# A decoder block in fp32: passes over consecutive tokens, and the steps between attention and experts in earlier half units

## The reference, cut to what matters

```python
x = layernorm(x + attention(x))             # 16 heads of 64, softmax over 1024 keys, Wp, bp
x = layernorm(x + memory(ctx, x))           # a shift of rows; 38 rows are a convolution of rate 4
x = layernorm(x + experts(x))               # top-1 of 8 experts, capacity 1024 / 8 tokens a batch

logits = einsum('bnd,de->bne', tokens, Wg); gates = softmax(logits)
mask = one_hot(argmax(gates), 8)
pos = cumsum(mask, axis=1) * mask - mask    # a token beyond its expert's capacity is dropped
h = gelu(expert_rows @ W1[e]); y = h @ W2[e]
```

## Time and profile before

| | |
|---|---|
| median of three runs | 2017.19 us |
| profiled execution, span | 2020.08 us, 2018.3 us |
| mean granted clock of TensorE | 0.967 |
| busy: PE, PEld, DVE, ACT, POOL | 94%, 62%, 59%, 43%, 68% |
| attention, tail | up to 1716.3 us, 302 us |
| PE waits for max_of (L1203), whole span | 30.8 us in 16 waits, the longest 6.9 |

### The profile page before, as it was taken

How to read it: one execution, slowest core, us unless ns; L and a number is a source line. 1 busy time by engine, 2 the same in 40 slices (tenths; PEclk the granted TensorE clock), 3 DMA queues, 4 the chain that set the end, 5 groups by cost and what they waited for, 6 DMA issues and landing times. The chain is left out here.

```text
span 2018.3 us, 30518 instructions
## 1 busy us (share of the span) xinstructions
PE 1896.4 (94%) x11400; PEld 1257.8 (62%) x11400; DVE 1198.5 (59%) x2123; ACT 865.5 (43%) x1118; POOL 1362.7 (68%) x725
## 2 busy tenths in 40 slices
PE   7899999999999999789999999899999997788996
PEld 5555666656666666456666665556666653777886
DVE  5555655656666656656666657656665675454563
ACT  3344444434434454234435443333344532446663
POOL 1687778778667776587667776686667767353553
PEclk8999999999999999899999999899999998887999
DMA  4300000022111100022102000211111101622330
GB/s 141 87 22 17 22 17 27 17 64 78 44 38 42 34 22 17 22 74 89 42 22 64 16 22 17 66 45 48 37 47 34 32 12 58 204 87 84 118 106 32
DMA packets 150093, 104.24 MB, mean 52 GB/s; under 512 B 74044, under 2 KB 136636, under 8 KB 148924
## 3 DMA queue, kind: packets, MB, share of 16 engines
q1 hardware_dynamic: 146876, 93.82, 15.9%
q0 software_dynamic: 3072, 8.46, 1.1%
HBM read 69.15 MB, written 29.43 MB: 49 GB/s over the span
## 5 line engine op out<-in xcount | busy, mean ns | idle before, releaser
L937 POOL TENSOR_TENSOR prob_sum<-prob_sum,probs 128x1024 f32<-128x1024 f32 x384 | 921.8, 2400 | 251.4 <-ACT probs L1147 223.4
L1203 DVE TENSOR_REDUCE max_of<-spare_ps 128x1 f32<-128x512 f32 x1024 | 656.7, 682 | 388.1 <-PE spare_ps L1030 387.5
L1147 ACT ACTIVATE probs<-score_ps 128x1024 f32<-128x1024 f32 x512 | 504.1, 1026 | 719.1 <-PE score_ps L1051 718.9
L1065 PE MATMUL av_ps<-probs,v 128*64 128x512 f32 x2048 | 488.6, 603 | 3.6 <-issue 3.6
L1030 PEld LDWEIGHTS spare_ps<-k_hi,q_hi 64*128 64x128 f32 x1024 | 160.2, 305 | 228.0 <-issue 191.6
L1030 PE MATMUL spare_ps<-k_hi,q_hi 64*128 64x512 f32 x1024 | 262.8, 507 | 31.5 <-DVE max_of L1203 30.8
L1065 PEld LDWEIGHTS av_ps<-probs,v 128*64 128x64 f32 x2048 | 130.4, 136 | 238.7 <-issue 221.6
L933 POOL TENSOR_TENSOR prob_sum<-probs 128x1024 f32<-128x1024 f32 x64 | 152.4, 2381 | 155.3 <-ACT probs L1147 155.3
L1051 PE MATMUL score_ps<-q_hi,k_hi 64*128 64x512 f32 x1024 | 213.2, 411 | 1.1 <-DVE o_in L1236 0.9
L1051 PE MATMUL score_ps<-shift_rows,ones 64*128 64x512 f32 x1024 | 207.3, 399 | 0.0
L1051 PE MATMUL score_ps<-q_hi,k_lo 64*128 64x512 f32 x1024 | 206.2, 396 | 0.0
(11 more groups left out here) (202 smaller groups left out, 2363.6 us busy)
## 6 DMA issues: line engine op xcount, KB each, us to landing
o_transposed<-o_out SPq DMA_DIRECT2D x64, 256.0 KB, 2.1
w_raw<-in_L_ffn_W_dram SPq DMA_DIRECT2D x16, 1024.0 KB, 5.6
o_in<-o_transposed SPq DMA_DIRECT2D x26, 512.0 KB, 4.0
w_raw<-in_L_attn_Wq_dram SPq DMA_DIRECT2D x64, 64.0 KB, 2.3
w_raw<-in_L_attn_Wk_dram SPq DMA_DIRECT2D x64, 64.0 KB, 2.2
wv_raw<-in_L_attn_Wv_dram SPq DMA_DIRECT2D x32, 128.0 KB, 2.8
x<-in_x_dram SPq DMA_DIRECT2D x4, 1024.0 KB, 6.0
xT_kept<-x_transposed SPq DMA_DIRECT2D x4, 1024.0 KB, 6.4
```

Source lines behind the costliest of these rows:

```text
L937: pool.tensor_tensor(out, out, probs[:, n % RING], ALU.add).then_inc(prob_added, 1)
L1065: last = pe.matmul(av_ps[hd * E:(hd + 1) * E, :], v[:, quad % 2, kt, 2 * first_head + hd, :], probs[:, n % RING, hd, :], start=(kt == 0), ...
L1147: act.activation(probs[:, n % RING], score_ps[n % 2][:, :, :], ACT.Exp).then_inc(probs_ready, 1)
L1203: dve.tensor_reduce(max_of[:, u % 2, kh, j, hd:hd + 1], bank[:, :], AX.X, ALU.max).then_inc(pass_read, 1)
```

## The change

Three parts. A pass takes 128 consecutive tokens as weights. The maxima then lie with the token along the partitions, so VectorE transposes them in blocks of 32 (neg_max, now 128 x 32 with zeros behind the eight used columns, into neg_rows, one buffer each) and four DMAs, one for each group of 32 partitions, write runs of 32 tokens into shift_rows. The route's projections come in the half units s = 4 to 11, and all that follows them three half units earlier. find_free and find_rows are cut into five pieces (kept, free, numbers, place, rows) in s = 26 to 28, and the sends stand in s = 29 and s = 30, four each.

```diff
@@ -167,7 +167,7 @@
         self.steps = 0
 
 
-    PROJECTED_AT = (5, 6, 7, 9, 10, 11, 13, 14)
+    PROJECTED_AT = (4, 5, 6, 7, 8, 9, 10, 11)
 
     def add_buffers(self, nc, ctx, more):
 
@@ -183,35 +183,39 @@
         early = {1: [("load_x", b)],
                  2: [("load_o", T0), ("load_o", T0 + 1), ("bias", b, 0)],
                  3: [("bias", b, 1)],
-                 15: [("load_cw", b), ("ids", b), ("load_new", b)],
-                 16: [("norm1", b, 4)],
-                 17: [("old", b), ("norm1", b, 0)],
-                 18: [("move", b), ("moved", b, 0)],
-                 19: [("moved", b, 1)],
-                 22: [("norm2", b, 0)],
-                 23: [("x2T", b, 0), ("norm2", b, 4)],
-                 24: [("x2T", b, 1)],
-                 25: [("x2T", b, 2)],
-                 26: [("x2T", b, 3)],
-                 27: [("choose", b)],
-                 28: [("tally", b)],
-                 29: [("count", b)],
-                 31: [("send", b, 0), ("send", b, 1)]}.get(s, [])
+                 12: [("load_cw", b), ("ids", b), ("load_new", b)],
+                 13: [("norm1", b, 4)],
+                 14: [("old", b), ("norm1", b, 0)],
+                 15: [("move", b), ("moved", b, 0)],
+                 16: [("moved", b, 1)],
+                 19: [("norm2", b, 0)],
+                 20: [("x2T", b, 0), ("norm2", b, 4)],
+                 21: [("x2T", b, 1)],
+                 22: [("x2T", b, 2)],
+                 23: [("x2T", b, 3)],
+                 24: [("choose", b)],
+                 25: [("tally", b)],
+                 26: [("count", b)],
+                 27: [("free", b)],
+                 28: [("place", b)],
+                 29: [("send", b, 0)],
+                 30: [("send", b, 1)]}.get(s, [])
         late = {3: [("split", T0)],
-                15: [("aggr", 0, b), ("scale", 0, b)],
-                16: [("norm1", b, 6)],
-                17: [("norm1", b, 2)],
-                19: [("comp", b), ("stats2", b, 0)],
-                20: [("stats2", b, 1)],
-                21: [("aggr", 1, b), ("scale", 1, b)],
-                22: [("norm2", b, 2)],
-                23: [("logits", b, 0), ("norm2", b, 6)],
-                24: [("logits", b, 1)],
-                25: [("logits", b, 2)],
-                26: [("logits", b, 3)],
-                27: [("mask", b)],
-                29: [("rows", b, 0)],
-                30: [("rows", b, 1)]}.get(s, [])
+                12: [("aggr", 0, b), ("scale", 0, b)],
+                13: [("norm1", b, 6)],
+                14: [("norm1", b, 2)],
+                16: [("comp", b), ("stats2", b, 0)],
+                17: [("stats2", b, 1)],
+                18: [("aggr", 1, b), ("scale", 1, b)],
+                19: [("norm2", b, 2)],
+                20: [("logits", b, 0), ("norm2", b, 6)],
+                21: [("logits", b, 1)],
+                22: [("logits", b, 2)],
+                23: [("logits", b, 3)],
+                24: [("mask", b)],
+                26: [("kept", b)],
+                27: [("numbers", b)],
+                28: [("rows", b)]}.get(s, [])
         for t in range(self.TB):
             early += [("load_o", T0 + t)] if t > 1 and s == (at[t - 3] + 1 if t > 2 else 4) else []
             late += [("proj", T0 + t)] if s == at[t] else []
@@ -559,7 +563,7 @@
         dve.tensor_copy(self.counts[:, :, :], bank[:, 0:(self.TB + 1) * self.EX]
                         .rearrange("p (t e) -> p t e", e=self.EX)).then_inc(self.counts_out, 1)
 
-    def find_free(self, dve, b):
+    def find_kept(self, dve, b):
         CAP, EX = float(self.CAP), self.EX
         base = self.base[:, b, :]
         in_tile, total = self.counts[:, 0:self.TB, :], self.counts[:, self.TB, :]
@@ -570,11 +574,17 @@
                           base.rearrange("p (a e) -> p a e", a=1).broadcast_to([P, self.TB, EX]), ALU.add)
         self.step(dve, dve.scalar_tensor_tensor(out=self.kept[:, :, :], in0=in_tile, scalar=CAP,
                                                 in1=self.mask[:, :, :], op0=ALU.is_lt, op1=ALU.mult))
+
+    def find_free(self, dve, b):
+        CAP, base = float(self.CAP), self.base[:, b, :]
         dve.tensor_scalar(self.free[:, :], self.taken[:, :], -1.0, CAP, ALU.mult, ALU.add)
         dve.tensor_tensor(self.free_row[:, :], self.taken[:, :], base, ALU.add)
         dve.tensor_reduce(self.dropped_before[:, :], self.dropped[:, :, :], AX.X, ALU.add)
         dve.tensor_reduce(self.keep[:, :], self.kept[:, :, :], AX.X, ALU.add)
         self.step(dve, dve.tensor_tensor(self.work[:, :, :], self.number[:, :, :], self.kept[:, :, :], ALU.mult))
+
+    def find_numbers(self, dve, b):
+        EX = self.EX
         dve.tensor_reduce(self.row[:, :], self.work[:, :, :], AX.X, ALU.add)
         dve.tensor_tensor(self.x2[:, :, self.GATE:self.GATE + 1], self.gate[:, :].rearrange("p (t a) -> p t a", a=1),
                           self.keep[:, :].rearrange("p (t a) -> p t a", a=1), ALU.mult)
@@ -583,8 +593,7 @@
                                          ALU.mult))
         self.step(dve, dve.tensor_reduce(self.free_before[:, :], self.triangle[:, :, :], AX.X, ALU.add))
 
-    def find_rows(self, dve, b):
-        tiles = slice(b * self.TB, (b + 1) * self.TB)
+    def find_place(self, dve, b):
         number, inside, work = self.number[:, :, :], self.inside[:, :, :], self.work[:, :, :]
         self.step(dve, dve.tensor_tensor(number, self.spread(self.dropped_before), self.over_tokens(self.free_before),
                                          ALU.subtract))
@@ -594,6 +603,9 @@
                                                 op0=ALU.is_ge, op1=ALU.mult))
         self.step(dve, dve.tensor_tensor(work, work, inside, ALU.mult))
         self.step(dve, dve.tensor_reduce(self.place[:, :], work, AX.X, ALU.add))
+
+    def find_rows(self, dve, b):
+        tiles = slice(b * self.TB, (b + 1) * self.TB)
         self.step(dve, dve.tensor_scalar(self.keep[:, :], self.keep[:, :], -1.0, 1.0, ALU.mult, ALU.add))
         self.step(dve, dve.tensor_tensor(self.place[:, :], self.place[:, :], self.keep[:, :], ALU.mult))
         self.step(dve, dve.tensor_tensor(self.row[:, :], self.row[:, :], self.place[:, :], ALU.add))
@@ -741,7 +753,8 @@
         inverse = sb("inverse", [P, BANK // BLOCK])
         o_out = sb("o_out", [P, 2, BANK])
         max_of = sb("max_of", [P, 2, 2, JT, 2])
-        neg_max = sb("neg_max", [P, 2, 2, JT], F32R)
+        neg_max = sb("neg_max", [P, BLOCK], F32R)
+        neg_rows = sb("neg_rows", [P, BLOCK], F32R)
         shift_rows = sb("shift_rows", [P, 2, BANK], F32R)
 
         score_ps = [ctx.enter_context(nc.psum_tensor(f"score_ps{i}", [P, 2, BANK], F32)) for i in range(2)]
@@ -779,6 +792,8 @@
         pass_ready = sem("pass_ready")
         pass_read = sem("pass_read")
         max_done = sem("max_done")
+        max_zeroed = sem("max_zeroed")
+        max_found = sem("max_found")
         shift_in = [sem(f"shift_in{i}") for i in range(2)]
         score_ready = sem("score_ready")
         probs_ready = sem("probs_ready")
@@ -818,9 +833,10 @@
             def move_shift(u):
                 sp.wait_ge(max_done, u + 1)
                 wait(sp, score_ready, KT * (u - 1))
-                for hd in range(2):
-                    sp.dma_start(shift_rows[hd * E:hd * E + 1, u % 2, :].rearrange("a (q j) -> a q j", j=JT).bitcast(F32),
-                                 neg_max[:, u % 2, hd, :].bitcast(F32)).then_inc(shift_in[u % 2], 16)
+                for r in range(P // BLOCK):
+                    rows = neg_rows[r * BLOCK:r * BLOCK + 2 * JT, :]
+                    heads = shift_rows[0:E + 1:E, u % 2, :].rearrange("h (j r i) -> h r j i", j=JT, i=BLOCK)
+                    sp.dma_start(heads[:, r].bitcast(F32), rows.bitcast(F32)).then_inc(shift_in[u % 2], 16)
 
             def store_o(u):
                 sp.wait_ge(o_done, u + 1)
@@ -943,6 +959,7 @@
             split_w(0)
             split_wv(0)
             split_w(1)
+            pool.memset(neg_max[:, :].bitcast(F32), 0.0).then_inc(max_zeroed, 1)
             pool.memset(prob_sum[:, 0, 0, 0:P], 1.0).then_inc(rows_zeroed, 1)
             pool.memset(o_out[:, :, :], 0.0).then_inc(rows_zeroed, 1)
             pool.wait_ge(rows_zeroed, 2)
@@ -1020,7 +1037,7 @@
 
                 par = u // 2 % 2
                 j, kh = divmod(i, 2)
-                tokens = slice(u % 2 * BANK + j, (u % 2 + 1) * BANK, JT)
+                tokens = slice(u % 2 * BANK + j * P, u % 2 * BANK + (j + 1) * P)
                 keys = slice(kh * BANK, (kh + 1) * BANK)
                 pe.wait_ge(bite_hi_done, max(NUMBER["q", u // 2, u % 2], NUMBER["k", u // 2, kh]) + 1)
                 n = 2 * PASS_NO["pass", u, i]
@@ -1037,7 +1054,7 @@
                 keys = slice(kt * P, (kt + 1) * P)
                 tokens = slice(u % 2 * BANK, (u % 2 + 1) * BANK)
                 if kt == 0:
-                    pe.wait_ge(shift_in[u % 2], 32 * (u // 2 + 1))
```

(28 more changed lines are left out.)

## The result

| | before | after |
|---|---|---|
| median (lowest to highest) of 4 runs on one chip | 2017.51 us (2015.80 to 2018.59) | 1994.70 us (1991.79 to 1995.65) |
| profiled execution, span | 2020.08, 2018.3 us | 1994.53, 1992.8 us |
| mean granted clock of TensorE | 0.967 | 0.968 |

The ratio is 0.9885, 95% interval 0.9868 to 0.9902: 1.15% faster. The forecast was 1976 us; the time lies inside its range (1945 to 2005), at the upper edge of the likeliest case's own (1958 to 1996). Of the 41 us forecast, 23 came.

What follows compares the result with a forecast made beforehand. TensorE, busy 94% of the span, was taken as the bound. Passes -27, two batches' choice and sends -21, third batch +7 made -41 us, from 2017.2 to 1976 us; eight-in-ten range 1945 to 2005.

Steps and rivals of the forecast that it cites:

- the likeliest case: Whole kernel: the main forecast of 1976 us, own range 1958 to 1996, chance 0.60.
- The load: Passes behind av or sum: consecutive tokens load weights faster, 0.12 us at 224 places, 27 us gained.
- The transposes at nothing: VectorE after a unit's last pass: 64 new transposes of 0.25 us, hidden by a wait for ScalarE; uncovered 16 us.
- What the choice and the sends cost before: s = 28, 29, 31 and next batch's s = 0, 2: 23.7 us a batch, in two batches.
- what they cost afterwards: New places of choice and sends, s = 12 to 31: steps less what TensorE forgives, 13.4 us a batch.
- the scales: Normalisation scales late in s = 12 and s = 18: 1.2 and 2.2 us a batch not forgiven.
- mask and tally: Mask late in s = 24 costs 2.1 us, tally early in s = 25 costs 1.6, a batch.
- Kept (1.6) and rows (1.5): Kept late in s = 26, bounds 0 to 2.3 us; rows late in s = 28, bounds 0.2 to 2.5.
- the slow clock: TensorE's lower clock after waits: 1.0 us a batch, less than 3.0 behind the 6.9 us wait, each wait being shorter.
- The third route: Third batch, choice in attention's last units: 9 us of new waits up to s = 27, 2 less at the end, +7.
- The rivals with other signs: Slower through GpSimd's chain, 2023 us, chance 0.05; little left, 2010 us, chance 0.05, of it 0.03 to no change.
- the pieces forgiven altogether: Rival: shorter VectorE pieces fall between GpSimd's adds, waits 3 us a batch or less; 1949 us, chance 0.22.

Runs made afterwards that it cites:

- e5_third_sends_in_tail: The changed kernel with the third batch's eight sends moved from s = 29 and 30 to the start of GpSimd's next block: 0.9837 of before, 1985.88 us.
- e8_stride_two: The changed kernel with a pass's weights taken as every second token, 8 bytes apart: one run, 1991.55 us.
- everything spread: The changed kernel with mask, tally, count, kept, the third batch's rows and all sends re-placed, its third-batch sends in the next block: 0.9792 of before, 1977.43 us.
- the tally later: The changed kernel with the tally late instead of early in s = 25, mask staying late in s = 24: 0.9943 of before, 2007.83 us.

## Why the prediction was right in sign and short by half in size

- **The load (27 us): right.** 26.4 us for the passes alone; the pair behind av 0.50 us, the load 187 ns. That run changes the transposes and the DMAs too; no run takes them apart, but the pair's 0.12 us at 224 places is the whole of it.
- **The transposes at nothing: right.** 64 of 0.21 us (0.25 taken) cost nothing that can be seen: the passes' 26.4 us are net of them.
- **What the choice and the sends cost before (23.7 us a batch), less what they cost afterwards (13.4): right with the old passes, in part by luck.** The route alone gave 10.4 and 10.1 us where 10.3 were forecast. By its half units the cost afterwards is 13.6 there, but out of other terms: the scales 2.2 (forecast 3.4), idle time of mask and tally 3.0 (3.7), the clock 3.1 (1.0). The last error hid the others. The cost before left out s = 30, 11.3 us at a clock of 0.94 where 10.6 is plain.
- **What they cost afterwards with the new passes (13.4 a batch): mis-sized.** Against the plain lengths of after, s = 25 costs 17.0 - 10.1 = 6.9, s = 27 16.1 - 14.4 = 1.7, s = 29 11.9 - 10.1 = 1.8, s = 0 15.3 - 11.1 = 4.2; with 0.8 idle in s = 12 and 1.5 in s = 18 and 19 that is 16.9 (and 1.5 more in the second batch of attention, in s = 19). Kept (1.6) and rows (1.5) were forecast well, both scales a little high (3.4 against 2.3). Idle time of mask and tally was forecast at 3.7 and is 4.2, that of the sends 2.0 and is 2.6. The term that failed is the slow clock, 1.0, "less than the 3.0 behind the wait of 6.9 us, since each wait is shorter". It is 6.9 - 4.2 = 2.7 in s = 25 and 4.2 - 2.6 = 1.6 in s = 0, 4.3 in all; over the six such batches of after, e5_third_sends_in_tail and e8_stride_two it is 4.4 to 6.0, s = 19 included. The wait of 2.6 us, less than half of the 6.9, still cost more than half as much in clock.
- **The two parts were summed as if they did not meet.** The choice's 21 us came to 20.5 with the old passes and to 13.2 with the new. The 7.3 us between them are made up of 4.1 in the two s = 0, 2.1 in the two s = 25 and 1.5 in the one slow s = 19, less some tenths elsewhere. What TensorE forgives was read at the old pass times. In s = 0 it is some 0.6 us less with quicker passes, in every join on record, and the lower clock goes with it in most. For s = 25 and s = 19 no such effect of the passes is shown: there executions with the same places differ by as much.
- **The third route (+7): mis-sized in the same term.** TensorE's idle time in h = 100 to 123 rose by 9.3 us, and 9 were forecast; the stretch against passes alone grew by 12.8. Most of the other 3.5 is again the lower clock (2.5 us in s = 25, at 0.81: 17.7 less 10.1 and 5.1 idle). The end was forecast at -2 and came to +0.6 up to the next block, inside its bounds: the sends left the end, and the last sum waits 11.0 us for them in place. Also in s = 29 TensorE's av waits 4.64 us; norm at 1644.75 stood behind the rows, and this was not in the forecast at all. That norm is what av waits for is read from the order of the rows; the release itself has no record. The wait is 1.5 when the rows stand a half unit later.
- Together, in spans: -26.8 for the passes alone, -13.2 and +13.4 for the route in company, +1.1 at the start and in the next block: -25.5, as measured. The medians differ by 22.8, because the profiled execution of before was 2.6 us above its median. The forecast's own upper end does not add up: 17 us more than 1976 are 1993, not 1996, and the time lies 2 us beyond that. The rivals with other signs did not occur, nor were the pieces forgiven altogether: TensorE is idle 1.4 us in s = 27, 1.3 in s = 29 and 4.2 in s = 25.

What stays open is when the clock falls. It is not settled by the wait alone: of the twelve joins with 2.4 to 2.7 us idle nine have the lower clock and three do not. Where s = 18 ends and s = 19 begins TensorE has one wait of 1.47 to 1.49 us in each of the 27 routes of after and of the eight runs with new passes and moved route. In 12 of them s = 19 then takes 16.8 or 16.9 us at 0.90, in 15 it takes 15.3 at 1.00; with the old passes the wait is 1.38, and all three stay at 1.00. One of the 12 is in after (the wait, and the stretch):

```profile
674.89 0.50 PE L1047 MATMUL spare_ps<-k_hi,q_hi 64*128 64x512 f32 x2 [1.48 <-DVE max_of L1220]
674.10:690.90 16.80, 15.96 (x86) 9.47 (x88) 7.24 (x13) 8.50 (x14) 9.47 (x4) 0.90 0.12 32
```

The runs show the levels and the waits, not the rule.

## What to carry to other kernels

Slack that a queue forgives is a difference of two times: when one part of a change makes the bound engine quicker, read the slack of every other part again at the new speed. Price a wait of TensorE as itself and add what the clock may take: here nothing behind waits of 1.2 to 1.35 us, 1.5 us behind 12 of 27 waits of 1.48, 1.1 to 3.3 us behind most of 2.4 us and more. So three waits of 1.3 us cost less than one of 4. Compare the same stretch in several executions before a difference of 1 to 2 us is put down to an edit. Move small dependent steps of VectorE to half units in which the list has room behind them, not merely to other half units. Work at the end of a block that no later step of the block needs belongs in the next block.

## What the runs showed of the hardware that was not expected

- A weight load of 64 x 128 fp32r takes 187 ns with neighbouring columns, 194 with columns 8 bytes apart, 305 with 16 bytes.
- All 44 waits of TensorE of 1.2 to 1.35 us in the routes of the first two batches (s = 24, 27 and 29, in ten runs) leave its granted clock at 1.00. Of 27 waits of 1.48 us (s = 19) 12 lower it, of twelve of 2.4 to 2.7 us (s = 0) nine, of twelve of 2.7 to 2.9 us (s = 25) all. One of 3.44 us left it at 1.00 (s = 0 behind the second batch, passes alone).
- What is lost beyond the wait follows its length only loosely: 1.4 to 1.8 us behind 2.4 to 2.7 in nine joins and 0.0 to 0.1 in the other three, 1.7 behind 3.8 (s = 2 of before), 1.1 behind 4.2 (s = 29 of before and the half unit after it), 2.7 to 3.3 behind 3.0 to 4.2 in two waits (s = 25). Behind the same wait of 6.9 us in s = 31 it is 3.0 in before and 1.8 with the passes alone (23.1 - 14.4 - 6.9).
- The same eight adds of 128 x 8 on VectorE take 1.57 to 1.69 us early in a half unit, and 5.35 and 6.00 late in one, beside GpSimd's adds (s = 24 with everything spread, s = 25 with the tally later); a single step of 0.2 us takes up to 2.3.
